# Hybrid attention and FFN block, Trainium2, one core: the out-projection of the heads as three f16 products, with the PSUM banks of keys and turned contexts exchanged

## The reference

```python
x = x + attn_a(layernorm(x))     # one wide head (1024), causal softmax, out-projection
x = x + ffn(layernorm(x))        # 64 units: s = x@Win + bin; relu(s*W1 + b1) . W2 + b2; @Wout + bout
x = x + attn_b(layernorm(x))     # 16 heads of 64, below
x = x + ffn(layernorm(x))

def attn_b(x):                   # the part that the change touches
    q, k, v = x @ Wq, x @ Wk, x @ Wv             # per head, 64 wide
    p = softmax(causal(q @ k.T / 8))
    heads = concat(p @ v)                        # 512 x 1024
    y = x + heads @ Wo
    return layernorm(y) * gamma + beta
```

## Time and profile before

| | |
|---|---|
| median of 3 runs | 880.51 us (880.41 to 880.76) |
| the profiled execution | 878.94 us, its span 877.1 us |
| TensorE busy | 728.0 us (83%) |
| VectorE busy | 665.4 us (76%) |
| ScalarE busy | 573.9 us (65%) |
| GpSimd busy | 520.9 us (59%) |

### The profile page before, as it was taken

One profiled execution on the slowest core, in us unless ns is written; L12 is line 12 of the kernel. 1 busy time (PEld: TensorE's weight loads), 2 busy tenths in 40 slices (PEclk: granted clock), 3 DMA queues, 4 the chain that ended last, 5 costly groups with the idle time before them and its releaser, 6 DMA issues. The chain is left out here.

```text
span 877.1 us, 21234 instructions
## 1 busy us (share of the span) xinstructions
PE 728.0 (83%) x7592; PEld 523.7 (60%) x7592; DVE 665.4 (76%) x1358; ACT 573.9 (65%) x1575; POOL 520.9 (59%) x496
## 2 busy tenths in 40 slices
PE   4376666642689999999999999999999999998842
PEld 3265555532457676766767766766776676676531
DVE  2478888875466668868987996898799689879873
ACT  0257666653367676677777777777777777777633
POOL 2156666462156567766785685667578566766831
PEclk9599778865799999999999999999999999999985
DMA  9011111100079988899898888889889889898820
GB/s 210 23 48 49 49 48 37 48 25 36 25 131 150 152 146 141 147 144 140 143 146 137 150 139 145 145 141 144 138 151 143 142 143 141 151 143 152 147 58 24
DMA packets 367142, 100.29 MB, mean 114 GB/s; under 512 B 347968, under 2 KB 364864, under 8 KB 367040
## 3 DMA queue, kind: packets, MB, share of 16 engines
q1 hardware_dynamic: 363776, 96.86, 64.3%
q10 hardware_dynamic: 3264, 2.10, 0.9%
HBM read 8.73 MB, written 2.10 MB: 12 GB/s over the span
## 5 line engine op out<-in xcount | busy, mean ns | idle before, releaser
L1031 POOL TENSOR_TENSOR prob_hl<-prob,prob_hl 128x768 f16<-128x768 f32 (+1 forms) x192 | 347.5, 1810 | 205.3 <-DVE prob_hl L971 205.1
L942 ACT ACTIVATE prob<-wide,neg_max 128x128 f32<-128x128 f32 (+3 forms) x512 | 264.5, 525 | 155.6 <-DVE neg_max L983 155.5
L983 DVE TENSOR_REDUCE neg_max<-wide 128x2 f32<-128x256 f32 (+3 forms) x256 | 204.3, 819 | 109.9 <-PE wide L860 108.6
L855 PE MATMUL wide<-k_sb,q_sb 64*128 64x128 f32 (+3 forms) x1024 | 190.1, 469 | 0.9 <-ACT k_sb L837 0.8
L971 DVE CAST prob_hl<-prob 128x768 f16<-128x768 f32 (+1 forms) x192 | 155.1, 808 | 0.9 <-DMA prob_t<-prob_hl 0.7
L880 PE MATMUL bank<-v_hi,prob_t 128*128 128x64 f16 x1280 | 132.2, 193 | 15.4 <-DMA prob_t<-prob_hl 13.2
L882 PE MATMUL bank<-v_hi,prob_t 128*128 128x64 f16 x1280 | 132.2, 193 | 0.0
L881 PE MATMUL bank<-v_lo,prob_t 128*128 128x64 f16 x1280 | 132.2, 193 | 0.0
L880 PEld LDWEIGHTS bank<-v_hi,prob_t 128*128 128x128 f16 x1280 | 115.3, 98 | 21.4 <-issue 16.2
L882 PEld LDWEIGHTS bank<-v_hi,prob_t 128*128 128x128 f16 x1280 | 113.9, 98 | 0.0
L881 PEld LDWEIGHTS bank<-v_lo,prob_t 128*128 128x128 f16 x1280 | 113.8, 98 | 0.0
(11 more groups left out here) (190 smaller groups left out, 1427.0 us busy)
## 6 DMA issues: line engine op xcount, KB each, us to landing
prob_t<-prob_hl SPq DMA_TRANSPOSE x384, 3.2
x_next<-in_L_attn_a_in_features SPq DMA_DIRECT2D x8, 256.0 KB, 3.0
x_attn<-in_L_attn_a_in_features SPq DMA_DIRECT2D x8, 256.0 KB, 3.3
x_sb<-x_done SPq DMA_DIRECT2D x8, 256.0 KB, 2.3
y_res<-bn_y SPq DMA_DIRECT2D x8, 256.0 KB, 2.3
out_x<-x_done SPq DMA_DIRECT2D x8, 256.0 KB, 2.6
wq_a<-in_L_attn_a_w_q ACTq DMA_DIRECT2D x1, 512.0 KB, 5.3
wq_b<-in_L_attn_b_Wq SPq DMA_DIRECT2D x1, 512.0 KB, 8.4
```

The source lines that it names most:

```text
L855: pe.matmul(dst[:, h, c:c + m], q[e, i * P:(i + 1) * P], k[e, 0:m], start=(i == UNIT_ROWS[u][0]), stop=False)
L942: last = act.activation(prob_2[s][:, at:at + m], score_banks(p, s)[:, h, c:c + m], ACT.Exp, bias=neg_max[p % 2][:, h, i:i + 1], accum_out= ...
L983: last = dve.tensor_reduce(neg_max[p % 2][:, :, i:i + 1], score_banks(p, s)[:, :, c:c + m], AX.X, ALU.max, negate=True)
L1031: pool.tensor_tensor(prob_hl[u][:, w:2 * w], prob_2[u][:, 0:w], prob_hl[u][:, 0:w], ALU.subtract)\
```

## The change

The output weights are scaled by their own largest element and split into f16 wo_hi and wo_lo; the turned context is split into f16 ctx_t_hi (ScalarE) and ctx_t_lo (VectorE, new, in slot 2 behind the row maxima); the out-projection is three f16 products per block in place of one fp32 product; the scale goes back in when y is summed (`back_sum_vector`). Contexts are turned into bank QK and keys are projected into bank MB, the reverse of before. v_lo moves in VectorE's slot 0 ahead of the cast, ScalarE's copy of the keys moves ahead of that of the context, and the waits of all that use QK or MB follow. In the drain the FFN additions come one slot later.

```diff
-        wo_up = sb("wo_up", [P, HP, P])
+        wo_hi = sb("wo_hi", [P, HP, P], F16)
+        wo_lo = sb("wo_lo", [P, HP, P], F16)
+        y_scale = sb("y_scale", [P, 1])
...
-        ctx_t = sb("ctx_t", [P, S])
+        ctx_t_hi = sb("ctx_t_hi", [P, S], F16)
+        ctx_t_lo = sb("ctx_t_lo", [P, S], F16)
...
+            act.wait_ge(sem("wo_b_scaled"), 1)
+            act.copy(wo_hi[:, :, :], wo_b[:, :, :]).then_inc(sem("wo_hi"), 1)
...
+            dve.tensor_reduce(largest[:, 2:3], wo_b[:, :, :], AX.XY, ALU.max, apply_absolute_value=True)\
+                .then_inc(sem("largest"), 1)
...
-            dve.tensor_scalar(wo_up[:, :, :], wo_b[:, :, :], scale_up[:, 1:2], None, ALU.mult)\
-                .then_inc(sem("wo_up"), 1)
+            dve.tensor_scalar(wo_b[:, :, :], wo_b[:, :, :], scale_down[:, 2:3], None, ALU.mult)\
+                .then_inc(sem("wo_b_scaled"), 1)
+            dve.tensor_tensor(y_scale[:, :], scale_up[:, 1:2], scale_up[:, 2:3], ALU.mult).then_inc(sem("y_scale"), 1)
...
+            dve.tensor_tensor(wo_lo[:, :, :], wo_b[:, :, :], wo_hi[:, :, :], ALU.subtract).then_inc(sem("wo_up"), 1)
...
         def values_tensor(pe, b, p):
             n = number(b, p)
-            if n < 2:
-                wait(pe, "v_lo", n + VSLICES)
-            wait(pe, "ctx_t", n - 1)
+            wait(pe, "k_sb", n + 2)
...
         def project_tensor(pe, b, p, parts, done):
             n = number(b, p)
-            wait(pe, *(("k_sb", n) if done == "q_ps" else ("q_sb", n + 1)))
+            if done == "q_ps":
+                wait(pe, "ctx_t_lo", n - 3)
+            else:
+                wait(pe, "k_sb", n)
+                wait(pe, "v_lo", min(max(n - 1, 0) + VSLICES, PAIRS))
...
-            split_product(pe, QK, parts[:, p, 0, :], parts[:, p, 1, :], xt_hi[:, at], xt_lo[:, at])\
+            split_product(pe, QK if done == "q_ps" else MB, parts[:, p, 0, :], parts[:, p, 1, :],
+                          xt_hi[:, at], xt_lo[:, at])\
                 .then_inc(sem(done), 1)
...
         def context_turn_tensor(pe, b, p):
             wait(pe, "ctx", n + 1)
-            wait(pe, "v_lo", min(n + 2 + VSLICES, PAIRS))
-            transposes(pe, MB, ctx_sb[:, :, :, :].rearrange("p a h e -> p (a h e)"), QB).then_inc(sem("ctx_t_ps"), 1)
+            wait(pe, "q_sb", min(n + 4, PAIRS))
...
+            transposes(pe, QK, ctx_sb[:, :, :, :].rearrange("p a h e -> p (a h e)"), QB).then_inc(sem("ctx_t_ps"), 1)
...
         def output_tensor(pe, b, p):
-            wait(pe, "ctx_t", n + 1)
+            wait(pe, "ctx_t_lo", n + 1)
...
-                last = pe.matmul(YA[:, i * P:(i + 1) * P], ctx_t[:, i * P:(i + 1) * P], wo_up[:, p, :],
-                                 start=(p == 0 and i == 0), stop=(p == HP - 1 and i == QB - 1))
+                blk = slice(i * P, (i + 1) * P)
+                pe.matmul(YA[:, blk], ctx_t_hi[:, blk], wo_hi[:, p, :], start=(p == 0 and i == 0), stop=False)
+                pe.matmul(YA[:, blk], ctx_t_hi[:, blk], wo_lo[:, p, :], start=False, stop=False)
+                last = pe.matmul(YA[:, blk], ctx_t_lo[:, blk], wo_hi[:, p, :], start=False,
+                                 stop=(p == HP - 1 and i == QB - 1))
...
         def heads_scalar(act, b, p):
+                if s == 1 and pair_exists(*later(b, p)):
+                    keys_scalar(act, *later(b, p))
                 if s == 1 and pair_exists(*earlier(b, p, 2)):
                     wait(act, "ctx_t_ps", n - 1)
                     wait(act, "y_ps", n - 2)
-                    act.copy(ctx_t[:, :], MB[:, :]).then_inc(sem("ctx_t"), 1)
-                if s == 1 and pair_exists(*later(b, p)):
-                    keys_scalar(act, *later(b, p))
+                    act.copy(ctx_t_hi[:, :], QK[:, :]).then_inc(sem("ctx_t"), 1)
...
         def heads_vector(dve, b, p):
+                if s == 2 and pair_exists(*earlier(b, p, 2)):
+                    wait(dve, "ctx_t", n - 1)
+                    wait(dve, "y_ps", n - 2)
+                    dve.tensor_tensor(ctx_t_lo[:, :], QK[:, :], ctx_t_hi[:, :], ALU.subtract)\
+                        .then_inc(sem("ctx_t_lo"), 1)
...
+                if s == 0:
+                    bv, pv = before
+                    if 0 <= bv < B - 1:
+                        values_vector(dve, bv + 1, pv, MB)
                 u = (s - 1) % NU
                 if pair_exists(*(before if s == 0 else (b, p))):
                     split_vector(dve, *(before if s == 0 else (b, p)), u)
...
-                if s == 0:
-                    bv, pv = before
-                    if 0 <= bv < B - 1:
-                        values_vector(dve, bv + 1, pv, MB)
...
         def bank_left(b, p):
-            return min(number(b, p) + 2, PAIRS)
+            return min(number(b, p) - 1, PAIRS)
...
-            wait(pe, "k_sb", bank_left(c + 1, 7))
+            wait(pe, "ctx_t_lo", bank_left(c + 1, 7))
```

More of the change, by code:

```diff
@@ L303, in prepare_vector @@
             dve.wait_ge(sem("wv_b_hi"), 1)
+            dve.wait_ge(sem("wo_hi"), 1)
+            dve.wait_ge(sem("wo_b_scaled"), 1)
+            dve.tensor_tensor(wo_lo[:, :, :], wo_b[:, :, :], wo_hi[:, :, :], ALU.subtract).then_inc(sem("wo_up"), 1)
             dve.tensor_tensor(wv_b_lo[:, :], wv_b[:, :, :].rearrange("p h e -> p (h e)"), wv_b_hi[:, :].bitcast(F32),
@@ L745, in adds_at @@
             k = (p - 1) * NU + s
-            if b == B and 0 < k <= J:
-                found.append((B - 2, k - 1))
+            if b == B and 1 < k <= J + 1:
+                found.append((B - 2, k - 2))
             return found
@@ L836, in keys_scalar @@
             wait(act, "s2", n - 1)
-            act.copy(k_sb[p % 2][:, :], QK).then_inc(sem("k_sb"), 1)
+            act.copy(k_sb[p % 2][:, :], MB).then_inc(sem("k_sb"), 1)
         def pair_scores(pe, b, p, u):
@@ L888, in context_turn_tensor @@
             wait(pe, "ctx", n + 1)
-            wait(pe, "v_lo", min(n + 2 + VSLICES, PAIRS))
-            transposes(pe, MB, ctx_sb[:, :, :, :].rearrange("p a h e -> p (a h e)"), QB).then_inc(sem("ctx_t_ps"), 1)
+            wait(pe, "q_sb", min(n + 4, PAIRS))
+            if b == B - 1 and p == HP - 2:
+                wait(pe, "g_xt", B - 1)
+            if b == B - 1 and p == HP - 1:
+                wait(pe, "g_s", B - 1)
+            transposes(pe, QK, ctx_sb[:, :, :, :].rearrange("p a h e -> p (a h e)"), QB).then_inc(sem("ctx_t_ps"), 1)
         def output_tensor(pe, b, p):
             n = number(b, p)
-            wait(pe, "ctx_t", n + 1)
+            wait(pe, "ctx_t_lo", n + 1)
             if p == 0:
@@ L1059, in back_sum_vector @@
             wait(dve, "y_res_in", 16 * B)
+            wait(dve, "y_scale", 1)
             tokens = y_res[:, seq(c), :]
-            dve.tensor_tensor(tokens, YA[:, :].rearrange("p (a d) -> p a d", d=P), tokens, ALU.add)\
+            dve.scalar_tensor_tensor(out=tokens, in0=YA[:, :].rearrange("p (a d) -> p a d", d=P),
+                                     scalar=y_scale[:, 0:1], in1=tokens, op0=ALU.mult, op1=ALU.add)\
                 .then_inc(sem("y_acc"), 1)
@@ L1164, in back_s_tensor @@
             wait(pe, "g_xt", c + 1)
-            wait(pe, "k_sb", bank_left(c + 2, 0))
+            wait(pe, "ctx_t_lo", bank_left(c + 2, 0))
             pe.matmul(QK[:, :], win2[:, :, :].rearrange("p a m -> p (a m)"), ffn_xt, start=True, stop=True)\
@@ L1172, in back_out_tensor @@
             wait(pe, "g_s", min(c + 2, B) if c != B - 2 else c + 1)
-            wait(pe, "k_sb", bank_left(c + 3, 1))
+            wait(pe, "ctx_t_lo", bank_left(c + 3, 1))
             for i in range(QB):
```

10 lines of the change are left out of this document (5 added, 5 removed).

## The result

The kernel with the change takes **902.95 us** (median of 4 runs, 902.33 to 905.72) against 880.63 (4 runs, 880.41 to 881.55): 1.0242 times as long, 95% interval 1.0223 to 1.0262. It is slower. The forecast was 900.0 in 883.5 to 907.5.

What follows compares the result with a forecast made beforehand. TensorE was taken to pace p = 0 to 2 and all of sequence 0, VectorE p = 3 to 5 of sequences 1 to 6. Terms: -7.1 + 13.2 + 11.4 + 1.3 + 0.7 = +19.5 us, median 900.0, range 883.5 to 907.5.

Steps and rivals of the forecast that it cites:

- C: VectorE's loop, steps p = 3 to 5: ctx_t_lo ahead of the cast delays ctx_sb, 19 x 0.60 = +11.4 us.
- A: Out-projection on TensorE: f16 products take 0.77 instead of 0.98 us, saving 0.21 in 34 TensorE-paced steps, -7.1 us.
- B: Three back pieces in bank QK (p = 7, 0, 1): TensorE waits 0.76 us each for ctx_t_lo, +13.2 us in all.
- +0.60 for each step: VectorE-paced steps: ctx_t_lo ahead of the first cast lengthens each by 0.60 us, 19 steps.
- costs nothing: VectorE's slot 0: v_lo ahead of the second cast falls in time that cast spends waiting anyway, cost 0.
- step p = 5 to 6 I take at nothing: GpSimd's add ffn_xb beside the delayed cast: no change, or 0.45 us gained in each of six steps if both could run.
- D: Before the front: VectorE gains wo_lo (1.14) and y_scale (0.15), delaying at_x_lo, +1.3 us.
- E: In the drain: one ctx_t_lo is on the path of the last y, +0.7 us.
- (1): Rival: TensorE's relief decides, 0.21 us in each of 61 pairs, ctx_t_lo done before TensorE asks; 869.7 us, chance 0.12.
- (2): Rival: B without C, v_lo's move resolves the longer cast and the 19 steps cost nothing; 884.6 us, chance 0.2.
- (3): Rival: nothing saved, the room fails or the f16 products still cost 0.98, A is 0; 907.1 us, chance 0.12.
- 0.13 stays: TensorE-paced steps: of VectorE's 0.94 us of room, v_lo takes 0.60 and the shorter out-projection 0.21, leaving 0.13.

## Why the prediction was right, and where it was not

**What bounds the kernel:** right, and the base of the rest. The split of the steps into TensorE's and VectorE's, read from the values product against ctx_sb, held: with the low part removed, TensorE's saving showed in p = 0 to 2 and not in p = 3; with it doubled, p = 3, 4 and 5 lost 0.60 each. The reading against ctx_sb also held for p = 5, which was put with p = 3 and 4 without rows of its own: before, TensorE's values product starts there 0.06 to 0.09 after the end of ctx_sb in sequences 1 to 4 (0.32 and 0.95 in 5 and 6, where it waited for something else). That the step rose by only 0.10 has another reason, under C.

**A, -7.1:** 0.77 for the group as worked out. The relief in p = 2 is 0.19. In sequence 0 it did not arrive: its steps p = 3 to 6 are 8.74, 9.42, 8.75, 9.23 where before each was 8.93. TensorE there waits (238 to 307 us):

```profile
PE bank L894 <- DMA prob_t<-prob_hl: 3.1, 4, 1.5
```

In before the same stretch has one such wait, of 1.3. With v_lo back in its old place p = 4 is 9.40 and p = 6 is 8.96, so v_lo is not the reason for the first of them; with the low part behind the cast p = 3 to 6 are 8.74 or 8.75 each, but p = 7 is 10.79. Why the transposes come later stays open.

**B, +13.2:** right in kind, place and nearly in size. Each wait of sequences 1 to 6 holds TensorE up by 0.85 where 0.76 was taken, those in p = 0 and 1 of sequence 7 by 1.6 (2.3 from mask to back piece in place of 0.65) where 1.5 was taken. Step p = 1 rose by 0.69, near to 0.85 less 0.21 of A; p = 0 by 0.24, near to 0.85 - 0.35 - 0.21.

**C, +11.4:** right mechanism, wrong distribution. ctx_sb does come 0.60 later in all three steps: it ends 4.67, 4.49 and 4.48 us after the first scores before (p = 3, 4, 5, median of sequences 2 to 6), and 5.26, 5.07 and 5.08 after. But the steps rose by 0.60, 0.39 and 0.10: 1.09 a sequence in place of 1.80. The step that failed is "+0.60 for each step", together with the one that v_lo's move "costs nothing": in p = 5 it gains. Before, v_lo stands behind ctx_sb and ahead of the row maxima of slot 1. VectorE in p = 5 of sequence 4, before and then with the banks exchanged alone:

```profile
581.49 0.63 DVE L1003 TENSOR_TENSOR ctx_sb<-bank,rsum 128x512 f32<-128x512 f32 x1
582.04 0.68 DVE L810 TENSOR_TENSOR v_lo<-bank,v_hi 128x512 f16<-128x512 f32 x1
...
583.42 0.93 DVE L983 TENSOR_REDUCE neg_max<-wide 128x2 f32<-128x768 f32 x1
```

```profile
580.62 0.63 DVE L1014 TENSOR_TENSOR ctx_sb<-bank,rsum 128x512 f32<-128x512 f32 x1
...
581.95 0.93 DVE L990 TENSOR_REDUCE neg_max<-wide 128x2 f32<-128x768 f32 x1
```

From ctx_sb to these maxima it is 1.93 and 1.33. The step fell from 9.46 to 9.03 with this alone, and rose from 9.56 to 10.01 when v_lo was put back in the changed kernel. So the low part costs 0.53 in p = 5, near to 0.60, and v_lo's move wins 0.43 of it back. In p = 4 the step of before varied between 8.98 and 9.44 in sequences 3 to 6, in part from other waits (in sequence 4 the values product came 0.53 after ctx_sb). In p = 3 the measured 0.60 needs v_lo's new place: with v_lo last and the low part present the step is 8.74, shorter than before, since GpSimd's low part, 0.6 later, takes at_y with it, and the cast gets ahead of it: before, at_y starts 0.05 ahead of the cast, with v_lo last 0.07 behind. So with the low part present the words that v_lo's move "costs nothing" are right for the sum of the three steps and for none of them: it costs 1.01 in p = 3 and wins 0.45 in p = 4 and in p = 5.

Two things made up for what was missing: p = 6 rose by 0.31, where "step p = 5 to 6 I take at nothing" (by 0.84 in sequence 3, by 0.07 to 0.24 in 4 to 6), and p = 7 by 0.81, where 0.55 was forecast. That sequences 3 to 6 came out at +11.8 for a forecast of +11.6 is therefore in part luck. The bounds 0 and 1.2 per step were not touched.

The rule that was weighed for p = 5 to 6, of the Trainium skill, "SBUF — State Buffer", section "Who interferes with whom" (the first to issue has the shared ports, the other blocks), forbade a gain of 0.45 there. None came, and the trace shows the waiting that was argued for. In sequence 5 the add begins first, at 676.06, and ends at 677.34; the cast of 128x768 begins at 676.63 and ends at 677.75, 1.12 long where the same form alone takes 0.55.

**D and E:** the front cost +1.4 (1.3). That the two agree so well is in part luck: the ten profiled kernels that have the front of the changed one reach the first scores between 236.6 and 239.3 us, the three that have the old one between 236.5 and 237.0. Steadier is the start of at_x_lo, which comes 1.0 to 1.6 us later in all ten. Sequence 7 and the drain together cost 5.5 (4.7). The end of the run, from the first scores of the last pair on, varies between 56 and 63 us from kernel to kernel, also where only banks were exchanged (60.9 against 56.2), so E's 0.7 can't be told apart; that the additions come a slot later there was not tried alone.

**The sum** is 3.9 us short on the spans (2.95 on the medians, since the median of before lies 1.57 above its profiled execution and that of after 0.62): 1.0 for sequence 0, 1.3 for sequence 1 (p = 4, 5 and 6 at 9.57, 9.57 and 9.56 against 9.34, 9.43 and 8.93, and p = 7 at 10.49 against 9.36), 0.5 for sequence 2, 0.2 for sequences 3 to 6, 0.8 for the last, 0.1 for the front. The term for sequence 1 was too small because I took for it what the later sequences lose; before the change its p = 7 was 0.19 to 1.17 shorter than theirs, so it had more to lose.

**The rivals.** (1) fell: TensorE is there before ctx_t_lo is at all 18 back pieces of sequences 1 to 7. (2) fell: the longer cast was not cured by v_lo's move, it ends 0.55 behind GpSimd as before, and steps p = 3 and 4 are longer. (3) fell in its main part, the 0.98 for the group; of its 7 us one came true. "0.13 stays" of VectorE's room in TensorE's steps: 0.14 is left in p = 0 to 2.

## What to carry to other kernels

A busy share of 98% in the heads' stage named TensorE as the bound, and yet the whole relief of TensorE was worth 2 us and one VectorE instruction of 0.68 cost over 20. Before costing a change, set the end of each engine's loop against the one wait that closes it, step by step, and cost the added instruction by its place: what stands behind it in its queue, and who in the same slot waits for its result. To split an operand takes work from TensorE and gives it to an engine that has to be shown to have room. And when an instruction is moved to the other side of the one that closes the loop, cost both sides: here v_lo's move won 0.43 behind ctx_sb in p = 5, and a forecast that looked only ahead of it missed that.
